# First tile's self-attention probabilities divided by their sums on GpSimd before they are turned, in a fused PixArt block with routed experts

## The reference

```
qkv = h @ w_qkv + b_qkv;  qkv = roll(qkv, -64, axis=1) -> windows of 128 tokens
scores = einsum('bnqhd,bnkhd->bnhqk', q, k) / sqrt(16)
attn   = softmax(scores, axis=-1)
o      = einsum('bnhqk,bnkhd->bnqhd', attn, v)
x      = x + (roll(o, 64) @ w_so + b_so) * g_msa
... top-16 cross-attention, x = x + (...) * g_mca
... MLP: x = x + (silu(a) * b @ w_m2 + b_m2) * g_mlp
... experts: x + sigmoid(...) * (sum_e router_e * (silu(c @ w1_e) @ w2_e) @ out_w + out_b)
```

## Time and profile before

| | value |
|---|---|
| runs | 1451.11 us median of 3 (1449.06 to 1451.4) |
| profiled execution, first to last instruction | 1447.1 us |
| TensorE busy | 1413.0 us, 98% |
| VectorE busy | 1061.7 us, 73% |
| ScalarE busy | 837.8 us, 58% |
| GpSimd busy | 437.8 us, 30% |
| chain that ended last | PE 83%, DVE 12%, issue 2%, ACT 1% |
| granted TensorE clock, mean | 0.994 of full |

### The profile page before, as it was taken

The page is one execution under the profiler, slowest core; times in us unless marked ns, Lnnn a source line. Parts: engine busy times, 40 slices in busy tenths (PEclk is TensorE's granted clock), DMA queues, the critical chain, the costliest instruction groups (busy, mean ns, idle before and its releaser), DMA issues.

```text
span 1447.1 us, 30246 instructions
## 1 busy us (share of the span) xinstructions
PE 1413.0 (98%) x9777; PEld 1195.1 (83%) x9777; DVE 1061.7 (73%) x4754; ACT 837.8 (58%) x2555; POOL 437.8 (30%) x599
## 2 busy tenths in 40 slices
PE   7999999999999999999999999999999999999997
PEld 5778788888888888888888788888888878887886
DVE  3585869688796878879696777959688786968642
ACT  3464475757566384755757466574757547574433
POOL 1314132333325232332335232233334313232302
PEclk9999999999999999999999999999999999999999
DMA  7520000010000000010010000000010000000000
GB/s 244 196 73 2 1 1 25 1 34 9 19 31 15 1 2 25 2 34 2 21 36 2 15 2 16 11 15 20 8 43 8 16 2 1 9 2 8 1 2 14
DMA packets 27342, 34.99 MB, mean 24 GB/s; under 512 B 3325, under 2 KB 22449, under 8 KB 26930
## 3 DMA queue, kind: packets, MB, share of 16 engines
q1 hardware_dynamic: 27185, 33.07, 7.1%
HBM read 28.83 MB, written 4.22 MB: 23 GB/s over the span
## 4 chain that ended last, share of the span: by engine, by line
PE 83%; DVE 12%; issue 2%; ACT 1%; SPq 0%; POOL 0%; DMA 0%; DVEq 0%; ACTq 0%; POOLq 0%
PE bank L965 13%; PE bank L920 12%; PE bank L989 10%; PE bank L972 7%; PE bank L791 6%; PE bank L929 6%; PE bank L777 4%; PE bank L852 4%; PE bank L840 4%; PE bank L904 4%; DVE knocked L2224 3%; PE bank L830 2%; PE bank L748 2%; PE bank L762 2%; PE bank L812 1%
## 5 line engine op out<-in xcount | busy, mean ns | idle before, releaser
L920 PE MATMUL bank<-hB,Wm 128*128 128x256 f32 x1024 | 242.3, 383 | 2.2 <-ACT hB L1366 2.2
L920 PEld LDWEIGHTS bank<-hB,Wm 128*128 128x128 f32 x1024 | 190.6, 190 | 33.4 <-issue 7.0
L965 PE MATMUL bank<-nxT,W1nx 128*128 128x256 f32 x896 | 212.1, 382 | 0.0
L1405 ACT ACTIVATE prob<-bank,rmax 128x128 f32<-128x128 f32 x512 | 180.3, 432 | 28.3 <-DVE rmax L2151 28.3
L1762 POOL TENSOR_TENSOR scores<-scores,M 128x308 f32<-128x308 f32 x128 | 94.5, 738 | 320.1 <-DVE knocked L2224 317.7
L1412 ACT ACTIVATE probT<-bank 128x512 f32<-128x512 f32 (+1 forms) x256 | 140.3, 617 | 83.8 <-PE bank L904 76.8
L989 PE MATMUL bank<-W2p,gT 128*128 128x256 f32 x768 | 183.2, 381 | 3.0 <-DVE acc L2303 1.9
L965 PEld LDWEIGHTS bank<-nxT,W1nx 128*128 128x128 f32 x896 | 166.1, 191 | 23.1 <-issue 2.8
L989 PEld LDWEIGHTS bank<-W2p,gT 128*128 128x128 f32 x768 | 141.2, 190 | 23.8 <-issue 2.8
L1450 ACT ACTIVATE tbs<-bank,b1half 128x256 f32<-128x256 f32 x128 | 60.7, 474 | 143.1 <-PE bank L920 102.2
L1466 ACT ACTIVATE tbs<-bank,betaH 128x256 f32<-128x256 f32 x224 | 95.6, 489 | 82.7 <-PE bank L972 82.7
(11 more groups left out here) (238 smaller groups left out, 2772.4 us busy)
## 6 DMA issues: line engine op xcount, KB each, us to landing
Wm_g<-in_L_xcond_w_m_dram SPq DMA_DIRECT2D x4, 1024.0 KB, 5.4
W1ev<-in_L_xcond_e_w_dram SPq DMA_DIRECT2D x6, 512.0 KB, 7.2
x<-in_x_dram SPq DMA_DIRECT2D x16, 128.0 KB, 2.6
x<-in_x_dram SPq DMA_DIRECT2D x32, 64.0 KB, 2.3
Wm<-in_L_xcond_w_m_dram SPq DMA_DIRECT2D x1, 2048.0 KB, 9.3
out_dram<-acc SPq DMA_DIRECT2D x16, 128.0 KB, 1.7
out_dram<-acc SPq DMA_DIRECT2D x32, 64.0 KB, 2.0
batch_rows<-row_store SPq DMA_DIRECT2D x4, 384.0 KB, 3.9
```

What stands on the lines that cost most here:

```text
L920: m = pe.matmul(bank_of(name)[:, half * UT:(half + 1) * UT], Wm1[:, k, c:c + P], hB[:, k, :], start=(k == 0), stop=(k == CB - 1))
L965: pe.matmul(bank_of(name)[:, n * UT:(n + 1) * UT], W1nx[:, k, c0 + n * P:c0 + (n + 1) * P], nxT[:, k, :], start=(n == 0 and k == 0), stop= ...
L1405: m = act.activation(prob[:, s, i, :], psum[s][:, i * P:(i + 1) * P], ACT.Exp, bias=rmax[:, t, s * HPS + i:s * HPS + i + 1], accum_out=rsu ...
```

## The change

Tile 0 is now handled as tile 1 is, but the multiplication is put on GpSimd:

- DVE inverts tile 0's sums slot by slot (`a_invert(0, s)`, four instructions of 128x4) at four places between its other work, in place of the one reciprocal of 128x16.
- GpSimd multiplies each slot's probabilities by the inverses (`a_weigh_first`, four instructions of 128x512), after `a_spread("xv")` and ahead of `b_mix_biases`. Its spreading of the inverses for `pv` goes.
- `a_turn_probs(0, s)` on PE now waits for that multiplication, and `b_second(0, (2, 3))` stands before the turning of slot 3 instead of behind it.
- The two transposes of the inverses on PE, their copy on ACT, and the separate handling of tile 0 in `a_values_out` go: DVE copies the whole bank at once. The job `r1` leaves the loop's table and stays in the prologue's alone (`PRO_BANK`).

```diff
-        def weighs_early(t, u):
-            return u >= 2 and t in EARLY
+        def weighs_early(u):
+            return u >= 2
@@ PE @@
             def a_turn_probs(t, s, u):
                 wait_drained(pe, f"s{t}{s}", u)
-                if weighs_early(t, u):
-                    pe.wait_ge(weighted, weighed(t, s, u))
+                if weighs_early(u):
+                    pe.wait_ge(weighted[t], weighed(s, u))
...
                 a_turn_probs(0, 2, a)
+                b_second(0, (2, 3), b)
                 a_turn_probs(0, 3, a)
-                b_second(0, (2, 3), b)
                 a_scores(1, range(SLOTS), a)
...
-                a_turn_inverses("r1", "pv", a)
                 a_values(1, a)
@@ ACT @@
-                a_copy_inverses("r1", "pv", a)
@@ GpSimd @@
+            def a_weigh_first(s, u):
+                g = slice(s * HPS, (s + 1) * HPS)
+                pool.wait_ge(slot_inverted[0], weighed(s, u))
+                alone(pool)
+                pool.tensor_tensor(prob[:, s], prob[:, s], rinv[:, 0, g].rearrange("p (i a) -> p i a", a=1).to_broadcast([P, HPS, P]),
+                                   ALU.mult).then_inc(weighted[0], 1)
...
                 a_spread("xv", c)
+                for s in range(SLOTS):
+                    a_weigh_first(s, a)
                 b_mix_biases(b)
                 if r == 0:
                     gate_b(batch)
-                a_spread("pv", a)
                 rstd_of(2, EPS0, c)
@@ DVE @@
             def a_values_out(dst, u):
                 wait_full(dve, "pv", u)
-                wait_drained(dve, "r1", u)
-                bk = bank_of("pv")[:, :].rearrange("p (f t) -> p f t", f=CB)
-                dve.tensor_copy(dst[:, :, P:UT], bk[:, :, P:UT])
-                dve.tensor_tensor(dst[:, :, 0:P], bk[:, :, 0:P], hA[:, :, 0:P], ALU.mult).then_inc(drained[JOB["pv"][0]], 1)
+                dve.tensor_copy(dst[:, :, :].rearrange("p f t -> p (f t)"), bank_of("pv")[:, :]).then_inc(drained[JOB["pv"][0]], 1)
...
                 a_max(0, (3,), a)
+                a_invert(0, 0, a)
                 b_route_norm(b)
                 a_residual(xc, xc, "co", c)
+                a_invert(0, 1, a)
                 b_silu("h10", hE[:, 1], 0, b)
+                a_invert(0, 2, a)
                 wait_drained(dve, "co", c)
                 ln_stats(2, xc, c)
+                a_invert(0, 3, a)
                 b_mix(0, b)
...
-                a_invert_sums(a)
```

More of the change, by code:

```diff
@@ L57 @@
 FIRST_ORDER = ["h00", "h01", "h10", "h11", "h20", "h21", "hg"]
+PRO_BANK = {"r1": 0}
 JOB = {name: (bank, i, len(jobs)) for bank, jobs in enumerate(BANK_JOBS) for i, name in enumerate(jobs)}
+JOB.update({name: (bank, None, None, None) for name, bank in PRO_BANK.items()})
 STAGE_C = {"xv", "r2", "co", "ln3"} | {f"{x}{t}{s}" for x in "cy" for t in range(TILES) for s in range(SLOTS)}
-STAGE_A = {"ln1", "k", "q", "v", "pv", "r1", "so", "ln2", "q2"} | \
+STAGE_A = {"ln1", "k", "q", "v", "pv", "so", "ln2", "q2"} | \
           {f"{x}{t}{s}" for x in "sp" for t in range(TILES) for s in range(SLOTS)}
-LEAD = {name: 1 if name in STAGE_A else 0 if name in STAGE_C else -1 for name in JOB}
+LEAD = {name: 1 if name in STAGE_A else 0 if name in STAGE_C else -1 for name in JOB if name not in PRO_BANK}
 PRO_JOBS = [
@@ L79 @@
 DEFERRED = {"e2": "m6", "g2": "y01"}
-for _jobs in BANK_JOBS:
+for _bank, _jobs in enumerate(BANK_JOBS):
     _n = 0
     for _name, _u in PRO_JOBS:
-        if _name in _jobs:
+        if _name in _jobs or PRO_BANK.get(_name) == _bank:
             PRO_ORDER[_name, _u] = _n
@@ L299, in bass_pixart_experts @@
         row_max = sem("row_max")
-        sums_inverted, slot_inverted, kept_inverted = sem("sums_inverted"), sem("slot_inverted"), sem("kept_inverted")
-        weighted = sem("probabilities_weighted")
+        sums_inverted, kept_inverted = sem("sums_inverted"), sem("kept_inverted")
+        weighted = [sem("first_tile_weighted"), sem("second_tile_weighted")]
+        slot_inverted = [sem("first_tile_inverted"), sem("second_tile_inverted")]
         spread_x = sem("kept_inverses_spread")
@@ L866, in a_turn_inverses @@
                 for f in range(CB):
-                    for t in range(1 if values == "pv" and u >= 2 else TILES):
+                    for t in range(TILES):
                         v = each[values][:, t, f * (H // CB):(f + 1) * (H // CB), :].rearrange("p h d -> p (h d)")
@@ L1415, in a_copy_inverses @@
             def a_copy_inverses(name, values, u):
[L1417 to L1421, removed]
                 copy_job(rT[values], name, u)
@@ L2523, in both @@
                 b_silu("h11", hE[:, 1], 2, b)
-                a_invert_sums(a)
-                a_weigh(1, 0, a)
-                a_weigh(1, 1, a)
-                a_weigh(1, 2, a)
-                a_weigh(1, 3, a)
+                a_weigh_second(0, a)
+                a_weigh_second(1, a)
+                a_weigh_second(2, a)
+                a_weigh_second(3, a)
                 ln_apply(2, xc, xnB, c)
```

24 lines of the change are left out of this document (11 added, 13 removed), and 2 rows, old and new, of the table BANK_JOBS.

## The result

| | before | after | ratio |
|---|---|---|---|
| median of 4 runs, us | 1450.09 (1447.06 to 1451.4) | 1477.56 (1475.5 to 1479.77) | 1.0194 [1.0173, 1.0215] |
| profiled span, us | 1447.1 | 1477.7 | |

The account below looks back on a forecast made before the run. PE was taken as the bound throughout the loop. Per pass 0.09 + 0.24 + 0.92 + 0.2 - 0.22 = 1.23 us, 17.2 over 14 passes, with 1.4 for the gates 18.6; 1451.1 + 18.6 gave 1470 us, range 1457 to 1486.

Parts of the forecast that it names:

- The read-out wait: Tile 1's scores on PE wait for ACT's copy of the last turned slot: 0.92 us a pass, bounds 0.75 and 1.1.
- The product: POOL's 128x512 multiplication of a slot's probabilities by the inverses: taken as 1.05 us, ends 1.0 and 1.4.
- Slot 0: Tile 0's first turning on PE waits 0.09 us a pass for POOL's multiplication.
- slot 2: Tile 0's third turning on PE waits 0.24 us a pass for POOL's multiplication.
- the reciprocal stands behind the residual, about 861.2: On DVE, slot 1's inverses come after the residual, at about 861.2 us in the timeline.
- Reciprocal done by 860.2, product 860.2 to 861.25: For tile 0's first slot, POOL's multiplication starts at 860.2 us, when DVE's inverses are done, and ends at 861.25.
- The collision: DVE's silu of h11 meets POOL's last bias sum, delaying tile 1's first turning: 0.2 us a pass taken, 0.43 if it waits.
- if the silu slips in, none: Case in which DVE's silu of h11 needn't wait for POOL's last bias sum: no wait ahead of tile 1's first turning.
- The transposes: Two transposes of inverses leave PE's chain: 0.22 us a pass saved, 14 x 0.22 = 3.1 us.
- The gates: In the three passes with r = 0, PE's so projection waits 0.4 to 0.5 us, bounds 0 and 2: 1.4 us.
- Which nothing here changes: The runs' median lies 4.0 us above the profiled span, and the change was said to leave that alone.
- GpSimd is the new bound: Rival: POOL's multiplications take 1.39 us each and hold up tile 0's turnings, 2.1 us a pass, 1483 us; 18%.

Follow-up runs that it names:

- swap_only: Kernel before, with one edit on PE: b_second(0,(2,3)) ahead of the turning of tile 0's slot 3; 1463.67 us, ratio 1.0112.
- route_first: Changed kernel with DVE's b_route_norm and a_invert(0,0) ahead of the last row maximum of tile 0; 1468.49 us, ratio 1.0132.
- swap_back_short: Changed kernel with PE's swap undone and the third expert's bias product and sum on POOL cut to 8 of 256 columns; 1464.04 us, ratio 1.0099.
- late_biases: Changed kernel with POOL's expert biases moved behind DVE's last product of tile 1, norm 2's deviation early and the gates last; 1487.48 us, ratio 1.026.
- no_division: Tile 0 left undivided in the loop, in PE's order of the kernel before, without the transposes and reciprocals; 1445.48 us, ratio 0.998.
- split: Changed kernel with b_second(0,(2,)) ahead of the turning of slot 3 and b_second(0,(3,)) behind it; 1469.46 us, ratio 1.0154.
- combined2: Changed kernel with late_biases, route_first, h20 and second layer reordered on PE, last bias sum and silus h21, hg later; 1448.74 us, ratio 1.0008.
- dve_products: Changed kernel with tile 0's products on DVE at the places of the reciprocals, POOL going straight to the biases; 1508.76 us, ratio 1.042.
- swap_back: Changed kernel with b_second(0,(2,3)) back behind the turning of slot 3; 1475.55 us, ratio 1.0199.

## Why the prediction was right, and where it was short

- **The read-out wait, 0.92 a pass.** Right: 1.38 less 0.44 is 0.94 in the timeline, and 0.85 net in the spacing of the scores (`b_second` takes 1.73 ahead of a turning, 882.49 to 884.22, where it took 1.82 ahead of the scores). It is the largest term, and swap_only shows it alone.
- **The product, 1.05 us.** Right: 1.04 where nothing stands beside it. The Trainium skill's GPSIMD Engine Reference (4.1 Engine selection) had put it at 1.39 by its factor of about two; against DVE's 0.693 the rows show 1.5, so the measurement decides.
- **Slot 0, 0.09, and slot 2, 0.24.** Mis-sized: 0.20 and 0.55, and 0.03 more in the step of PE behind each of the two, 0.81 together. For slot 2 the step that failed is "the reciprocal stands behind the residual, about 861.2". I had the silu take turns with POOL but not the six-column `rp`, which stands ahead of the residual. It takes 0.96 instead of 0.17, and the reciprocal of slot 1 comes later by that. route_first shows it: with `rp` moved, slot 2's wait is gone. For slot 0 `rp` has no part, since it starts behind that product. There the step "Reciprocal done by 860.2, product 860.2 to 861.25" left out the handover from DVE to POOL: the reciprocal ends at 877.48 and the product starts at 877.66, 0.18 later. These two terms are 0.47 a pass short, 6.6 us.
- **The collision, 0.2 (bounds 0 and 0.43).** The mechanism was right and the size short: 0.31, and 0.62 with r = 0. The silu met the last sum in every pass, so the case "if the silu slips in, none", for which the term had been halved, never occurred. The extra with r = 0 isn't the sum's: there the gates follow on POOL, and DVE's product beside them takes 1.01 instead of 0.69. swap_back_short and late_biases take the collision away and tile 1's turning comes at 5.65 (with r = 0 only where the gates are away too, as in late_biases).
- **The transposes, −0.22.** Right: −0.21 (8.38 to 8.17), and no_division measures their 3 us by themselves.
- **The gates, 1.4 us in three passes.** Cost nothing, by a tie. POOL's delay was there, as DVE's longer wait for the deviation shows (3.79 us, where the earlier trace rows had 2.76), but PE, held up more than forecast at the waits before, came at the very moment at which the read-out was done. Timeline in a pass with r = 0:

```profile
806.91 0.74 DVE L2136 TENSOR_SCALAR xnB<-x,mv,rstd 128x256 f32<-128x256 f32 x2 [3.79 <-POOL rstd L1750]
807.57 0.68 DVE L2178 COPY hA<-bank 128x512 f32<-128x512 f32 x1
...
806.57 1.99 PE L967 MATMUL bank<-nxT,W1nx 128*128 128x256 f32 x8
808.40 1.96 PE L793 MATMUL bank<-Wso_g,hA 128*128 128x256 f32 x8
```

The copy ends at 808.25, and PE starts 0.15 later, 1.83 behind its step before, as it does with no wait. In split, where PE would come 0.8 us earlier in the pass, the wait is there. Its row in that kernel's view of waits:

```profile
PE bank L793 <- DVE hA L2179: 1.6, 3, 0.5
```

By the spacing of starts it is 0.69 in each of the three passes.

- **The sum.** 18.6 forecast, 25.0 in the loop: 6.6 too little for slots 0 and 2, 2.4 for the collision (13 x 0.11 and 1.0), 1.0 for the read-out too much (14 x 0.07), 1.4 for the gates too much, and 0.6 by which the rests shrank; that makes 24.6. Most of the rest is that the loop, as measured here, holds the gain of the transposes 13 times and not 14.
- **"Which nothing here changes", of what lies around the loop.** Not quite so. Windows over 20 to 40 us (columns as in the earlier trace rows; the third last is the granted clock), first before:

```profile
20.00:40.00 20.00, 20.00 (x125) 13.12 (x127) 9.40 (x27) 11.38 (x43) 0.93 (x2) 0.91 0.62 200
```

after:

```profile
20.00:40.00 20.00, 20.00 (x111) 13.80 (x110) 8.30 (x24) 9.80 (x40) 0.93 (x2) 0.83 0.63 197
```

The mean granted clock of that stretch, between the levels of 1.2 and 2.4 GHz, was 0.91 before, 0.83 in the profiles of after, swap_only and no_division, and 1.00 in route_first and combined2. The instructions there are the same. From the span's start to the loop it is 181.3 us before, 183.8 after, and 179.5 and 179.9 in the last two, so I compare loops. Why it falls so is open; the profiled executions are one each.
- **Luck in the total.** The span grew by 30.6 us, 12.0 more than the sum: 6.4 in the loop and 5.6 around it. The median is only some 8 us above the sum's 1469.7, because the 4.0 by which it lay above the profiled span before was no constant: after, it lies 0.1 below (the profiled execution, at 1479.48, was one of the two longer ones of four). The terms of the loop are what the forecast can be judged by.

Of the rivals, *GpSimd is the new bound* came closest in time (1483), by the wrong reason: its 0.58 for slot 2 is near the 0.55 measured, but its 1.39 per product was not there, and dve_products goes against it. What was there is the turn-taking of POOL and DVE. The rule of the Trainium skill's SBUF — State Buffer (Who interferes with whom), that a DVE instruction with two SBUF inputs and a GpSimd instruction that reads SBUF exclude one another for a whole instruction, fits `rp` (blocked until POOL's product ends), the silu (1.72, 1.45) and the product on DVE (1.23). I had applied it to two silus, of h10 and h11, and not to `rp`. It is a coupling between the two queues besides the semaphores, which the description of the chip at the top calls the only one.

## What to carry to other kernels

When work goes to an engine that takes turns with another at SBUF, as POOL and DVE did here, list every instruction of that other engine which reads two SBUF operands in the same stretch, however small: the six-column product was held up by nearly the whole 1.04 us of the product beside it. When two steps of the bound engine are swapped to hide one wait, ask what the moved step had hidden: here 1.8 us of matmuls had covered a read-out, and their loss cost four times what the transposes gave. Before the work, bound the gain by leaving the step out: in this order 0.2% was all there was.

## What the hardware showed that I had not expected

- A DVE product of 128x6 takes 0.166 us alone and 0.964 beside a POOL product, a factor of 5.8, and it was the largest single error of the sum.
- The exclusion has no favourite: POOL's sum went from 1.27 to 1.60 when DVE was first, and DVE's silu from 0.68 to 1.72 when POOL was.
- Two kernels with different waits of PE (after and swap_back) took 18.40 us to the same point, because there one chain over POOL and DVE set the time in both. By PE's own chain the changed kernel would have been there at 18.10 (12.46 + 5.64), and swap_back at 17.80. So the part of a mended wait on PE that reached beyond 18.40 counted for nothing, until the scores came early enough for the silu to pass POOL's last sum (split, 17.93) or that sum went (swap_back_short, 17.81).
